# Splitting the attention maxima on GpSimd instead of VectorE, in a layer of attention and experts

## The chip, the cores and the metric

One core of a Trainium2 chip runs the whole program. The metric is the device time of one execution in microseconds (us); lower is better. The engines have their own instruction queues and meet through semaphores: TensorE (PE; its weight loads have a row of their own, PEld), VectorE (DVE), ScalarE (ACT), GpSimd (POOL), and SyncE (SP), whose queue here only issues DMAs.

## The reference

The input is 8 batches of 256 tokens with 128 channels. The layer is

```python
xn = layernorm(x)
out = x + attention(xn) + ffn(xn)
# attention: 16 heads of width 8, rotary q and k, softmax(q k^T / sqrt(8)) v, output projection
# ffn: xn + shared_mlp(xn) + the 2 best of 16 experts by a sigmoid router, weights normalised
# mlp: (silu(x @ wg) * (x @ wu)) @ wd, inner width 64
```

Everything is float32. The kernel keeps that accuracy on TensorE by cutting numbers into parts: a product of fp32r halves takes three matmuls, and q and k are each cut into three bf16 parts (six products, 48 rows for a head of width 8).

## The kernel before, in words

**Blocks.** The work is ordered by hand in blocks, `blk` from -6 to 33, each with four places `i` = 0 to 3. A block handles a quarter of a batch's heads, `q` (4 heads, one for each `i`), in three steps that lie apart: at block `q - 4` the scores are computed once to find their row maxima (`max_scores`, L488, into the two PSUM banks S1a and S1b; DVE reduces them at L903 into `mx`); at block `q` they are computed again for the exponentials (`exp_scores`, L502, into S2a and S2b; ACT takes the exponential at L657 into `probs`); at block `q + 1` the probabilities are multiplied with v (`attend`, L516). Between these lie one of 36 chunks of the expert network (two experts of a group of two batches): `up` into the banks FA and FB (L375 to L377), tanh on ACT (L669), two products on DVE (L914 into `th`, L895 into `gu`), the router's weight on POOL (L984, `gu` by `wbc`), the high part on ACT (L690, `hid_hi`), the low part on POOL (L1000, `hid_lo`), and in the next block `down` into the bank Y. Rotary sums, their splits, transpositions, projections and the router of each group are placed at blocks of their own by tables at the head of the file.

**The maxima.** The maximum must be subtracted ahead of the exponential. The kernel does this inside the second score product: `q_hat` has six more rows, which hold minus the maximum in three bf16 parts, against rows of ones in `k_hat`. A half, `h`, is two quarters (8 heads, 256 queries), so 16 maxima for each of 128 partitions. `negated_half(blk)` names the half whose last maximum was found in block `blk - 1`; it is one for each even block from -2 to 28. At that block DVE runs the four stages of `negate_maxima`, one behind the maximum of each place `i`:

- i = 0, L791: `md` part 0 = bf16(-m)
- i = 1, L794: `mrest` = -m - part 0
- i = 2, L797: part 1 = bf16(`mrest`)
- i = 3, L800: part 2 = `mrest` - part 1, and the semaphore `md_ready` rises.

Each waits until the one before is done. `md` and `mrest` are single buffers; `mx` holds two batches.

**What follows.** At place 0 of the next block (`transposed_half`) PE waits for `md_ready`, transposes `md` (L477) into the S1 bank that is next in turn, and DVE copies the 24 rows out as `mT` (L807). SP then issues the load of these rows into `q_hat` (`load_max`, L325), and at the block behind that `exp_scores` reads them. SP's queue is in order, so this load stands in one line with the loads of the heads (L318), the writes of the parts (L303) and the loads of router weights (L338, 2 MB a group).

**The order on POOL in a block:** weighting of `gu`, then at some blocks the low part of xT (L970) and a residual (L966), then at 14 places a rope split (five instructions on 128x256, L253 to L262), then `hid_lo`, and at four blocks the sum of the output (L1008). On ACT `hid_hi` stands ahead of the exponential of place 2. On PE, `max_scores` needs the S1 bank that DVE read two maxima ago.

Of the kernel before, what the change touches and what calls it, by code (L numbers as in the profile page):

```python
# [14 lines left out]
NQ = 4  # L15
# [10 lines left out]
PARTS = 3  # L26
# [49 lines left out]
def late_a(blk):  # L76

    return [(kind, of) for kind, blocks in LATE_A.items() for of, at in blocks.items() if at == blk]
# [7 lines left out]
def negated_half(blk):  # L86

    return blk // 2 + 1 if blk % 2 == 0 and blk // 2 + 1 in range(2 * B) else None


def transposed_half(blk):

    return negated_half(blk - 1)
# [38 lines left out]
def layer_kernel(nc, x, wqk, wv, bias, wout, gate_w, gate_b, swg, swu, swd, ewg, ewu, ewd,  # L132
                 cos, sin, ident, identb, iota, kones, out):
    f32, f32r, bf16, u32 = mybir.dt.float32, mybir.dt.float32r, mybir.dt.bfloat16, mybir.dt.uint32
    ALU = mybir.AluOpType
    ACT = mybir.ActivationFunctionType
    AX = mybir.AxisListType
    A_USE, B_USE, S_USE = bank_uses()
# [7 lines left out]
    with ctx:  # L146
        def sb(name, shape, dt=f32):
            return ctx.enter_context(nc.sbuf_tensor(name, shape, dt))
# [4 lines left out]
        def sem(name):  # L153
            return ctx.enter_context(nc.semaphore(name))
# [29 lines left out]
        mx = sb("mx", [P, 2, 2, SB, 2, NQ])  # L184
        mrest = sb("mrest", [P, SB * 2 * NQ])
        md = sb("md", [P, SB, 2, PARTS, NQ], bf16)
# [23 lines left out]
        stage = wbc[:, 1].rearrange("p c t -> p (c t)")  # L210
# [19 lines left out]
        md_ready = sem("md_ready")  # L230
        s1_ready, s1_read, s2_ready, exp_done = sem("s1_ready"), sem("s1_read"), sem("s2_ready"), sem("exp_done")
# [8 lines left out]
        def chunk_group(n):  # L240
            return n // NCH, n % NCH
# [460 lines left out]
        def _(dve):  # L702
            steps = [0]

            def step(instruction):

                steps[0] += 1
                instruction.then_inc(dve_step, 1)

            def settled():  # L710

                dve.wait_ge(dve_step, steps[0])
# [67 lines left out]
                                                  ALU.mult))  # L780
                    nc.vector.tensor_tensor(wtok[:], wsel[:, :, 0, :], wsel[:, :, 1, :], ALU.add).then_inc(wtok_ready, 1)

            def negate_maxima(h, stage):

                slot, half = (h // 2) % 2, h % 2
                m = mx[:, slot, half].rearrange("p t r j -> p (t r) j")
                part = [md[:, :, :, k, :].rearrange("p t r j -> p (t r) j") for k in range(PARTS)]
                left = mrest[:].rearrange("p (a j) -> p a j", j=NQ)
                if stage == 0:
                    dve.wait_ge(s1_read, S_USE["max", 2 * NQ * (h + 1) - 1] + 1)  # L790
                    step(nc.vector.tensor_scalar(part[0], m, -1.0, None, ALU.mult))  # L791
                elif stage == 1:
                    settled()
                    step(nc.vector.scalar_tensor_tensor(left, m, -1.0, part[0], ALU.mult, ALU.subtract))  # L794
                elif stage == 2:
                    settled()
                    step(nc.vector.tensor_copy(part[1], left))  # L797
                elif stage == 3:
                    settled()
                    nc.vector.tensor_tensor(part[2], left, part[1], ALU.subtract).then_inc(md_ready, 1)  # L800

            def maxima_to_rows(h):
                if h >= 2:
                    dve.wait_ge(max_ld[(h - 2) % 4], 16 * ((h - 2) // 4 + 1))
# [76 lines left out]
            for blk in range(FIRST, LAST + 1):  # L881
                n, q = blk + CHLEAD, blk + LEAD
                for g in range(1, G):
                    if NORMALISE_BLOCK.get(g) == blk:
                        normalise(g)
                for i in range(NQ):
                    if i == 0 and 0 <= n - 1 < NCHUNKS:

                        m = n - 1
                        rows = I if m % NCH == 0 else P  # L890
                        dve.wait_ge(fb_ready, B_USE["hu", m] + 1)
                        dve.wait_ge(fa_read, A_USE["hg", m] + 1)
                        if m >= 2:
                            dve.wait_ge(hid_ready, m - 1)
                        nc.vector.tensor_tensor(gu[0:rows, m % 2, :], FB[0:rows, :], th[0:rows, m % 2, :],  # L895
                                                ALU.mult).then_inc(fb_read, 1)
                    if i == 3:
                        for kind, g in late_a(blk):
                            read_a(kind, g)
                    if 0 <= q < NBLK:  # L900
                        use = S_USE["max", q * NQ + i]
                        dve.wait_ge(s1_ready, use + 1)
                        nc.vector.tensor_reduce(mx[:, (q // QB) % 2, (q // 2) % 2, :, q % 2, i],  # L903
                                                S1[use % 2][:].rearrange("p (t s) -> p t s", t=SB),
                                                axis=AX.X, op=ALU.max).then_inc(s1_read, 1)
                    if negated_half(blk) is not None:
                        negate_maxima(negated_half(blk), i)
                    if i == 0 and transposed_half(blk) is not None:
                        maxima_to_rows(transposed_half(blk))
                    if i == 0 and n < NCHUNKS:  # L910

                        rows = I if n % NCH == 0 else P
                        dve.wait_ge(th_ready, n + 1)
                        nc.vector.scalar_tensor_tensor(th[0:rows, n % 2, :], th[0:rows, n % 2, :], 1.0,  # L914
                                                       FA[0:rows, :], ALU.add, ALU.mult).then_inc(fa_read, 1)
                    if i == 1:
                        for kind, g in early_b(blk):
                            read_b(kind, g)
                    for g, stage in route_stages(blk, i):
                        route(g, stage)  # L920
# [3 lines left out]
        def _(pool):  # L924
            steps = [0]

            def after(instruction):

                steps[0] += 1
                instruction.then_inc(pool_step, 1)  # L930
                pool.wait_ge(pool_step, steps[0])
# [17 lines left out]
            def split_batch(w, g, slot):  # L949
# [3 lines left out]
                for stage in range(SPLIT_STAGES):  # L953
# [5 lines left out]
                    if stage < SPLIT_STAGES - 1:  # L959
                        pool.wait_ge(parts_done[slot], PARTS * (2 * g + w) + PART_STAGES.index(stage) + 1)  # L960

            def residual(g):
                pool.wait_ge(xn_ready, NTB * (g + 1))
                if g >= 2:
                    pool.wait_ge(out_done, 16 * (g - 1))
                nc.gpsimd.tensor_tensor(resid[:, g % 2], x_sb[:, g], xn[:, g % 2], ALU.add).then_inc(resid_ready, 1)  # L966
# [6 lines left out]
            for blk in range(FIRST, LAST + 1):  # L973
                n = blk + CHLEAD
                m = n - 1
                if 0 <= m < NCHUNKS:
                    g, c = chunk_group(m)
                    pool.wait_ge(fb_read, B_USE["hu", m] + 1)
                    if c == 0:
                        nc.gpsimd.tensor_scalar(gu[0:I, m % 2, :], gu[0:I, m % 2, :], 0.5, 1.0,  # L980
                                                ALU.mult, ALU.mult).then_inc(gu_weighted, 1)
                    else:
                        pool.wait_ge(wbc_ld[0 if c - 1 < WFIRST else 1], 32 * (g + 1))
                        nc.gpsimd.tensor_tensor(gu[:, m % 2, :], gu[:, m % 2, :], wbc[:, g % 2, c - 1, :],  # L984
                                                ALU.mult).then_inc(gu_weighted, 1)
                if blk == FIRST + 1:
                    xt_low(1)
                for kind, g in late_a(blk):
                    if kind == "G1":
                        xt_low(g)  # L990
                for g in range(G):
                    if blk == RESIDUAL_BLOCK[g]:
                        residual(g)
                for (g, w, slot), at in SPLIT_BLOCK.items():
                    if blk == at:
                        split_batch(w, g, slot)
                if 0 <= m < NCHUNKS:
                    rows = I if m % NCH == 0 else P
                    pool.wait_ge(hid_hi_ready, m + 1)
                    nc.gpsimd.tensor_tensor(hid_lo[0:rows, m % 2, :], gu[0:rows, m % 2, :],  # L1000
                                            hid_hi[0:rows, m % 2, :].bitcast(f32), ALU.subtract).then_inc(hid_ready, 1)
                for kind, g in early_b(blk):
                    if kind == "O2":
                        pool.wait_ge(fb_read, B_USE[kind, g] + 1)
                        flat = resid[:, g % 2].rearrange("p t c -> p (t c)")

                        pool.wait_ge(fa_read, A_USE["O1", min(GB * g + 1, B - 2)] + 1)
                        nc.gpsimd.tensor_tensor(flat, flat, y_tok[:], ALU.add).then_inc(o_ready, 1)  # L1008
# [61 lines left out]
```

## Time and profile before

| | |
|---|---|
| median of 3 runs | 259.78 us (257.04 to 262.89) |
| profiled execution, span | 260.4 us (no other time is given for it) |
| mean granted TensorE clock | 0.938 of full speed |
| TensorE busy | 220.3 us, 85% |
| VectorE busy | 204.7 us, 79% |
| ScalarE busy | 140.6 us, 54% |
| GpSimd busy | 157.3 us, 60% |
| DMA | 26.5 MB, mean 102 GB/s |

Busy time counts an instruction from its start to its end, also where it waits inside for something else. Instructions of one engine can overlap by up to about 0.1 us, since the next starts while the last drains. The chain that ended last is one path through the program, followed back from the end; its pieces are cut so that they don't overlap.

### The profile page before, as it was taken

The page shows a single profiled execution, that of the slowest core. Times are in us where ns is not written, and L with a number is a line of the kernel's source. Part 1 is how long each engine was busy: PE and PEld are TensorE (multiplying, and loading weights), DVE is VectorE, ACT ScalarE, POOL GpSimd, SP SyncE. Part 2 cuts the span into 40 slices and gives each one's busy share as a digit, 9 for nine tenths or more (in the row PEclk, how much of TensorE's full clock was granted, in tenths as well). Part 3 has the DMA queues.
Part 4 walks back from the last instruction along what each step waited for, and adds up shares of the span by engine and source line. Part 5 has one row for each costly group of instructions (what it writes and reads, how often), then busy time and mean ns, then how long its engine had stood idle before and what let it go on. Part 6 is the DMA issues. An engine that isn't in the chain of part 4 may idle for free.

```text
span 260.4 us, 4728 instructions
## 1 busy us (share of the span) xinstructions
PE 220.3 (85%) x1612; PEld 142.1 (55%) x1612; DVE 204.7 (79%) x468; ACT 140.6 (54%) x262; POOL 157.3 (60%) x167
## 2 busy tenths in 40 slices
PE   0572499879798986999988989999999899999973
PEld 0340265455465652666656556666766566776641
DVE  5889749949999782799996988999889789986301
ACT  2543132215566741566557656565767566676761
POOL 9299427498783545394783747469955374436711
PEclk9995569968999995999999999999999999999998
DMA  7902559440053795020235981201589611000101
GB/s 235 352 5 62 168 139 207 120 121 1 15 166 94 193 201 96 3 62 0 84 107 127 211 242 36 62 0 37 159 184 198 208 49 35 4 2 3 42 3 40
DMA packets 35183, 26.51 MB, mean 102 GB/s; under 512 B 3468, under 2 KB 29388, under 8 KB 35148
## 3 DMA queue, kind: packets, MB, share of 16 engines
q1 hardware_dynamic: 34456, 25.29, 38.4%
q10 hardware_dynamic: 704, 0.92, 1.0%
q8 instruction: 13, 0.21, 0.3%
q14 instruction: 10, 0.08, 0.1%
HBM read 18.53 MB, written 7.47 MB: 100 GB/s over the span
## 4 chain that ended last, share of the span: by engine, by line
PE 45%; DVE 26%; DMA 14%; SPq 7%; issue 5%; ACT 2%; POOL 1%; DVEq 0%; POOLq 0%
PE PV L516 8%; DVE mx L903 7%; DMA wbc<-route_w 5%; DMA q_hat<-mT 5%; PE S2b L502 4%; PE S2a L502 4%; PE S1a L488 3%; PE S1b L488 3%; PE Y L375 2%; SPq L303 2%; PE FA L376 2%; PE FA L375 2%; PE FA L377 2%; DVE xn L743 2%; PE Y L377 2%
## 5 line engine op out<-in xcount | busy, mean ns | idle before, releaser
L1000 POOL TENSOR_TENSOR hid_lo<-gu,hid_hi 128x512 fp32r<-128x512 f32 (+1 forms) x36 | 46.1, 1281 | 40.3 <-ACT hid_hi L690 40.2
L984 POOL TENSOR_TENSOR gu<-gu,wbc 128x512 f32<-128x512 f32 x32 | 40.9, 1277 | 30.3 <-DVE gu L895 22.6
L657 ACT ACTIVATE probs<-S2b 128x512 f32<-128x512 f32 x64 | 38.3, 599 | 35.0 <-PE S2b L502 34.9
L903 DVE TENSOR_REDUCE mx<-S1a 128x2 f32<-128x512 f32 x65 | 44.3, 681 | 13.2 <-PE S1a L488 13.0
L657 ACT ACTIVATE probs<-S2a 128x512 f32<-128x512 f32 x64 | 38.4, 600 | 22.3 <-PE S2a L502 20.3
L903 DVE TENSOR_REDUCE mx<-S1b 128x2 f32<-128x512 f32 x63 | 42.9, 681 | 4.9 <-PE S1b L488 4.7
L516 PE MATMUL PV<-probs,vx 128*32 128x256 f32 x512 | 35.6, 392 | 1.3 <-ACT probs L657 1.3
L669 ACT ACTIVATE th<-FA 128x512 f32<-128x512 f32 (+1 forms) x36 | 21.5, 597 | 22.0 <-PE FA L377 21.8
L690 ACT ACTIVATE hid_hi<-gu 128x512 fp32r<-128x512 f32 (+1 forms) x36 | 22.7, 632 | 13.9 <-POOL gu L984 12.7
L502 PE MATMUL S2a<-q_hat,k_hat 102*128 102x256 bf16 x128 | 25.4, 280 | 5.4 <-DMA q_hat<-mT 5.3
L914 DVE SCALAR_TENSOR_TENSOR th<-th,FA 128x512 f32<-128x512 f32 (+1 forms) x36 | 24.4, 677 | 5.8 <-ACT th L669 5.4
L895 DVE TENSOR_TENSOR gu<-FB,th 128x512 f32<-128x512 f32 (+1 forms) x36 | 24.5, 681 | 5.0 <-PE FB L377 4.9
L488 PE MATMUL S1a<-k_hat,q_hat 96*128 96x256 bf16 x130 | 25.8, 280 | 2.9 <-DVE mx L903 2.4
L488 PE MATMUL S1b<-k_hat,q_hat 96*128 96x256 bf16 x126 | 25.0, 280 | 0.8 <-DVE mx L903 0.5
L502 PE MATMUL S2b<-q_hat,k_hat 102*128 102x256 bf16 x128 | 25.2, 279 | 0.0
L375 PE MATMUL FA<-xT_hi,wg_hi 128*128 128x512 f32 (+1 forms) x36 | 18.3, 508 | 4.4 <-DVE th L914 2.3
L516 PEld LDWEIGHTS PV<-probs,vx 128*32 128x32 f32 x512 | 15.4, 110 | 12.1 <-ACT probs L657 6.1
L375 PE MATMUL FB<-xT_hi,wu_hi 128*128 128x512 f32 (+1 forms) x36 | 18.0, 500 | 3.5 <-ACT sig L615 3.2
L375 PE MATMUL Y<-hid_hi,wd_hi 128*128 128x512 f32 (+1 forms) x36 | 17.6, 490 | 1.8 <-POOL hid_lo L1000 1.8
L502 PEld LDWEIGHTS S2a<-q_hat,k_hat 102*128 102x128 bf16 x128 | 9.6, 100 | 17.1 <-DMA q_hat<-mT 6.6
L502 PEld LDWEIGHTS S2b<-q_hat,k_hat 102*128 102x128 bf16 x128 | 8.6, 98 | 18.5 <-issue 16.0
L488 PEld LDWEIGHTS S1a<-k_hat,q_hat 96*128 96x128 bf16 x130 | 11.8, 100 | 7.9 <-DVE mx L903 3.9
(128 smaller groups left out, 449.0 us busy)
## 6 DMA issues: line engine op xcount, KB each, us to landing
wbc<-route_w SPq DMA_DIRECT2D x8, 768.0 KB, 10.2
q_hat<-q_parts SPq DMA_DIRECT2D x32, 96.0 KB, 2.4
k_hat<-k_parts SPq DMA_DIRECT2D x32, 96.0 KB, 2.4
wbc<-route_w SPq DMA_DIRECT2D x8, 256.0 KB, 4.0
k_parts<-parts SPq DMA_DIRECT2D x8, 192.0 KB, 2.6
q_parts<-parts SPq DMA_DIRECT2D x8, 192.0 KB, 2.2
x_sb<-in_x SPq DMA_DIRECT2D x4, 256.0 KB, 4.0
q_parts<-parts SPq DMA_DIRECT2D x8, 128.0 KB, 2.1
```

The source lines that it names most:

```text
L375: nc.tensor.matmul(bank, w_hi, m_hi, start=start, stop=False)
L488: last = nc.tensor.matmul(bank[:, t * T:(t + 1) * T], q_hat[0:MROW, slot, pair, t * P:(t + 1) * P], k_hat[0:MROW, slot, pair, r, :], start ...
L502: last = nc.tensor.matmul(S2[head % 2][:, s * T:(s + 1) * T], k_hat[0:KALL, slot, pair, r, s * P:(s + 1) * P], q_hat[0:KALL, slot, pair, : ...
L516: last = nc.tensor.matmul(PV[32 * j:32 * j + 32, hg * T:(hg + 1) * T], vx[:, (b // GB) % 2, SB * (b % GB) + s, r, NQ * hg + j, :], probs[: ...
L657: nc.scalar.activation(probs[:, head % (2 * NQ), :], S2[head % 2][:], ACT.Exp, scale=SCALE).then_inc(exp_done, 1)
L669: nc.scalar.activation(th[0:rows, n % 2, :], FA[0:rows, :], ACT.Tanh, scale=0.5).then_inc(th_ready, 1)
L690: nc.scalar.activation(hid_hi[0:rows, (n - 1) % 2, :], gu[0:rows, (n - 1) % 2, :], ACT.Copy).then_inc(hid_hi_ready, 1)
L895: nc.vector.tensor_tensor(gu[0:rows, m % 2, :], FB[0:rows, :], th[0:rows, m % 2, :], ALU.mult).then_inc(fb_read, 1)
L903: nc.vector.tensor_reduce(mx[:, (q // QB) % 2, (q // 2) % 2, :, q % 2, i], S1[use % 2][:].rearrange("p (t s) -> p t s", t=SB), axis=AX.X, ...
L914: nc.vector.scalar_tensor_tensor(th[0:rows, n % 2, :], th[0:rows, n % 2, :], 1.0, FA[0:rows, :], ALU.add, ALU.mult).then_inc(fa_read, 1)
L984: nc.gpsimd.tensor_tensor(gu[:, m % 2, :], gu[:, m % 2, :], wbc[:, g % 2, c - 1, :], ALU.mult).then_inc(gu_weighted, 1)
L1000: nc.gpsimd.tensor_tensor(hid_lo[0:rows, m % 2, :], gu[0:rows, m % 2, :], hid_hi[0:rows, m % 2, :].bitcast(f32), ALU.subtract).then_inc(hi ...
```

## The change

The four stages leave DVE's queue. GpSimd gets `negate_maxima(h)` as the first thing in an even block, ahead of the weighting of `gu`. It has five instructions, since each of them is one plain product or sum: part 0 = bf16(-m); rest = m + part 0; part 1 = bf16(-rest); rest = rest + part 1; part 2 = bf16(-rest). The parts are the same in value. Each waits for the one before (`after`), and the last raises `md_ready`. It waits for the last maximum of the half and for the transposition of the half before, which read `md`. DVE gets a wait ahead of the first maximum of a half, for the split of the half whose place in `mx` it overwrites, four halves back.

```diff
--- before.py
+++ after.py
@@ -780,25 +780,6 @@
                                                   ALU.mult))
                     nc.vector.tensor_tensor(wtok[:], wsel[:, :, 0, :], wsel[:, :, 1, :], ALU.add).then_inc(wtok_ready, 1)
 
-            def negate_maxima(h, stage):
-
-                slot, half = (h // 2) % 2, h % 2
-                m = mx[:, slot, half].rearrange("p t r j -> p (t r) j")
-                part = [md[:, :, :, k, :].rearrange("p t r j -> p (t r) j") for k in range(PARTS)]
-                left = mrest[:].rearrange("p (a j) -> p a j", j=NQ)
-                if stage == 0:
-                    dve.wait_ge(s1_read, S_USE["max", 2 * NQ * (h + 1) - 1] + 1)
-                    step(nc.vector.tensor_scalar(part[0], m, -1.0, None, ALU.mult))
-                elif stage == 1:
-                    settled()
-                    step(nc.vector.scalar_tensor_tensor(left, m, -1.0, part[0], ALU.mult, ALU.subtract))
-                elif stage == 2:
-                    settled()
-                    step(nc.vector.tensor_copy(part[1], left))
-                elif stage == 3:
-                    settled()
-                    nc.vector.tensor_tensor(part[2], left, part[1], ALU.subtract).then_inc(md_ready, 1)
-
             def maxima_to_rows(h):
                 if h >= 2:
                     dve.wait_ge(max_ld[(h - 2) % 4], 16 * ((h - 2) // 4 + 1))
@@ -899,12 +880,12 @@
                             read_a(kind, g)
                     if 0 <= q < NBLK:
                         use = S_USE["max", q * NQ + i]
+                        if i == 0 and q % 2 == 0 and q >= 8:
+                            dve.wait_ge(md_ready, q // 2 - 3)
                         dve.wait_ge(s1_ready, use + 1)
                         nc.vector.tensor_reduce(mx[:, (q // QB) % 2, (q // 2) % 2, :, q % 2, i],
                                                 S1[use % 2][:].rearrange("p (t s) -> p t s", t=SB),
                                                 axis=AX.X, op=ALU.max).then_inc(s1_read, 1)
-                    if negated_half(blk) is not None:
-                        negate_maxima(negated_half(blk), i)
                     if i == 0 and transposed_half(blk) is not None:
                         maxima_to_rows(transposed_half(blk))
                     if i == 0 and n < NCHUNKS:
@@ -959,6 +940,21 @@
                     if stage < SPLIT_STAGES - 1:
                         pool.wait_ge(parts_done[slot], PARTS * (2 * g + w) + PART_STAGES.index(stage) + 1)
 
+            def negate_maxima(h):
+
+                slot, half = (h // 2) % 2, h % 2
+                m = mx[:, slot, half].rearrange("p t r j -> p (t r) j")
+                part = [md[:, :, :, k, :].rearrange("p t r j -> p (t r) j") for k in range(PARTS)]
+                left = mrest[:].rearrange("p (a j) -> p a j", j=NQ)
+                pool.wait_ge(s1_read, S_USE["max", 2 * NQ * (h + 1) - 1] + 1)
+                if h:
+                    pool.wait_ge(s1_ready, S_USE["M", h - 1] + 1)
+                after(nc.gpsimd.tensor_scalar(part[0], m, -1.0, 1.0, ALU.mult, ALU.mult))
+                after(nc.gpsimd.tensor_tensor(left, m, part[0], ALU.add))
+                after(nc.gpsimd.tensor_scalar(part[1], left, -1.0, 1.0, ALU.mult, ALU.mult))
+                after(nc.gpsimd.tensor_tensor(left, left, part[1], ALU.add))
+                nc.gpsimd.tensor_scalar(part[2], left, -1.0, 1.0, ALU.mult, ALU.mult).then_inc(md_ready, 1)
+
             def residual(g):
                 pool.wait_ge(xn_ready, NTB * (g + 1))
                 if g >= 2:
@@ -973,6 +969,8 @@
             for blk in range(FIRST, LAST + 1):
                 n = blk + CHLEAD
                 m = n - 1
+                if negated_half(blk) is not None:
+                    negate_maxima(negated_half(blk))
                 if 0 <= m < NCHUNKS:
                     g, c = chunk_group(m)
                     pool.wait_ge(fb_read, B_USE["hu", m] + 1)
```

## Rows read from the trace of the kernel before

**Rows 1.** the page, engine shares: PE and DVE, then the chain by engine
```profile
PE 220.3 (85%) x1612; PEld 142.1 (55%) x1612; DVE 204.7 (79%) x468; ACT 140.6 (54%) x262; POOL 157.3 (60%) x167
...
PE 45%; DVE 26%; DMA 14%; SPq 7%; issue 5%; ACT 2%; POOL 1%; DVEq 0%; POOLq 0%
```

**Rows 2.** by stretches; busy PE, PEld, DVE, ACT, POOL, clock, DMA
```profile
220.00:240.00 20.00, 20.00 (x174) 13.80 (x172) 16.28 (x33) 13.44 (x25) 10.18 (x8) 1.00 0.01 3
```

**Rows 3.** chain of waits, 60 to 69 us; columns start, length, what
```profile
61.58 0.79 DVE md L791
...
63.72 0.60 DVE mrest L794
```

**Rows 4.** chain of waits, 128 to 138 us
```profile
130.32 0.79 DVE md L791
...
134.37 1.17 DVE md L800
```

**Rows 5.** chain of waits, 168 to 174 us
```profile
168.55 0.79 DVE md L791
...
173.18 0.60 DVE md L797
```

**Rows 6.** chain of waits, 192 to 204 us
```profile
192.87 1.20 DVE md L791
...
196.54 0.86 DVE md L800
...
198.82 4.08 DMA q_hat<-mT
```

**Rows 7.** groups by line and shape, DVE; busy us, mean ns, idle
```profile
L791 DVE TENSOR_SCALAR md<-mx 128x16 bf16<-128x16 f32 x16 | 9.2, 573 | 0.0
L800 DVE TENSOR_TENSOR md<-mrest,md 128x16 bf16<-128x16 f32 x16 | 7.7, 483 | 0.0
...
L794 DVE SCALAR_TENSOR_TENSOR mrest<-mx,md 128x16 f32<-128x16 f32 x16 | 4.0, 247 | 0.0
...
L797 DVE CAST md<-mrest 128x16 bf16<-128x16 f32 x16 | 3.7, 229 | 0.0
```

**Rows 8.** timeline of POOL, 128 to 136 us; columns start, length, what
```profile
131.86 0.40 POOL L257 TENSOR_SCALAR parts<-rope 128x256 bf16<-128x256 f32 x1
132.34 0.67 POOL L259 TENSOR_TENSOR rest<-rope,parts 128x256 f32<-128x256 f32 x1
...
134.22 1.28 POOL L1000 TENSOR_TENSOR hid_lo<-gu,hid_hi 128x512 fp32r<-128x512 f32 x1
```

**Rows 9.** waits, all; columns who, for whom: us in total, times, longest
```profile
PEld S1a L477 <- DVE md L800: 4.3, 6, 1.7
...
PEld S1a L488 <- DVE mx L903: 3.9, 6, 1.3
...
PE S1a L477 <- DVE md L800: 1.7, 2, 1.3
```

**Rows 10.** groups by line and shape, POOL
```profile
L259 POOL TENSOR_TENSOR rest<-rope,parts 128x256 f32<-128x256 f32 x14 | 9.5, 679 | 1.2
...
L257 POOL TENSOR_SCALAR parts<-rope 128x256 bf16<-128x256 f32 x14 | 5.9, 422 | 1.2
...
L980 POOL TENSOR_SCALAR gu<-gu 64x512 f32<-64x512 f32 x4 | 2.5, 612 | 5.4 <-DVE gu L895 5.4
...
L934 POOL MEMSET gateb_sb<- 128x1 f32 x1 | 0.1, 98 | 0.0
```

**Rows 11.** timeline of POOL, the weighting in block 2 and in block 12
```profile
72.77 1.28 POOL L984 TENSOR_TENSOR gu<-gu,wbc 128x512 f32<-128x512 f32 x1 [0.32 <-DVE gu L895]
...
145.43 1.28 POOL L984 TENSOR_TENSOR gu<-gu,wbc 128x512 f32<-128x512 f32 x1
```

**Rows 12.** timeline of ACT, hid_hi in block 2 and in block 12
```profile
76.34 0.62 ACT L690 ACTIVATE hid_hi<-gu 128x512 fp32r<-128x512 f32 x1
...
146.74 0.63 ACT L690 ACTIVATE hid_hi<-gu 128x512 fp32r<-128x512 f32 x1 [0.90 <-POOL gu L984]
```

## The prediction

> **What bounds the kernel now.** The page first: TensorE (PE) is busy 85% of the span, VectorE (DVE) 79%, GpSimd (POOL) 60%, and the chain that ended last is 45% PE, 26% DVE, 1% POOL [rows 1]. So no engine is the bound alone. PE has the most to do, and DVE holds it up in places. In the table by stretches PE is filled completely from 220 to 240 us [rows 2]: there a faster DVE buys nothing. The chain of waits, read stretch by stretch, then says where DVE is the one that is late, and the four instructions that the change removes stand in it by name: 0.79 and 0.60 us between 60 and 69 us, 0.79 and 1.17 between 128 and 138, 0.79 and 0.60 between 168 and 174, 1.20 and 0.86 between 192 and 198 [rows 3 to 6]. Together that is 6.8 us; what else of them stands in the chain is small.
>
> Why should an instruction on 16 elements take a microsecond? The four have means of 573, 247, 229 and 483 ns, 64 instructions, 24.6 us of DVE in all [rows 7]. The long ones are waiting. The last of the four stands in the chain from 134.37 for 1.17 us, so it ends at 135.54 [rows 4]. POOL's 128x512 subtraction, begun at 134.22, took 1.28 and ended at 135.50 [rows 8]. DVE got on when POOL let go. The Trainium skill, "SBUF — State Buffer", section "Who interferes with whom", says that GpSimd and a DVE instruction that has two SBUF inputs (or runs in a two-port mode) hold one pair of ports as an exclusive lock, so that the second fully blocks; the trace agrees, by 1.17 us against POOL's end 0.04 us earlier. DVE's big instructions beside it read PSUM, and are not in this list.
>
> **The change, part by part.**
>
> *Removed from DVE.* 16 times (one for each half of a batch's heads) four instructions, and their places in the queue: the last stood behind the fourth maximum of an even block, and PE's transposition of the parts waits for it at the beginning of the next. What is that worth in time? Lower bound: the matmuls of that transposition stood idle for the last part 1.7 us in 2 places; the later of PE's two clocks on this, the weight loads, waited 4.3 us in 6 places [rows 9]. Upper bound for this term: all the big pieces of the chain, 6.8 us. I take 4.3: PE has the most work, so what PE can give is its waiting and not all of DVE's, and weight loads show a wait that the modelled end of a matmul covers. The two are not far from one another, and 4.3 lies between 1.7 and 6.8. Gain 4.3, ends 1.7 and 6.8.
>
> *Added on POOL.* Three one-input and two two-input instructions on 16 elements, each waiting for the one before. No such size is in the trace. Two-input: 679 ns for 256 elements, 1,280 for 512 [rows 8, 10], so 2.35 ns an element and about 115 ns at 16. One-input: 422 ns for 256 to bf16, 612 for 512 [rows 10], which would leave 240 ns at 16; the shortest POOL instruction of all takes 98 [rows 10]. I take the middle, 170. A dependent one starts 0.08 us after the end of the one before (131.86 + 0.40 = 132.26, next 132.34) [rows 8]. Sum: 3 x 0.17 + 2 x 0.115 + 4 x 0.08 = 1.06 us for a split. Ends: 5 x 0.098 + 0.32 = 0.8, and, if 16 elements cost what 256 do to bf16, 5 x 0.42 + 0.32 = 2.4 us.
>
> What is behind it on POOL: the weighting of gu, then ACT's hid_hi, which stands in ACT's queue ahead of the exponentials of the third and fourth pair, for which PE waits. The split begins when the last maximum of the block before is read, and in that same moment DVE begins gu, which takes 0.60 of the queue, and for which POOL has to wait anyway. So the weighting is late by 1.06 - 0.60 = about 0.5 us, and by all 1.06 where POOL comes late itself. In block 2 the weighting ends at 74.05 and hid_hi starts at 76.34 [rows 11, 12]: 2.3 us of cover, and 0.5 costs nothing. In block 12 POOL came late (it starts at 145.43 without idle time) and ACT waited 0.90 us for it [rows 11, 12]: there 1.06 us goes to the exponentials. I count half of it, 0.5, since PE has maxima and projections to do meanwhile; ends 0, and 2.1 for two such blocks with nothing hidden. The same POOL delay pushes the hid_lo subtraction and, in eight of the even blocks, the rope splits behind it; their readers (the down products, the scratch writes of SP's queue) come in general a block later, and stay covered as long as a block is over 5 us.
>
> *Waits.* POOL's new wait for the previous transposition was fulfilled a block ago. DVE's new wait before the first maximum of a half is for a split four halves back: nothing. SP's queue issues what it did, in its order; its load of the rows waits for the transposition, which comes no later. Cost of all these: 0, and under 0.1 if I am wrong in one.
>
> *A rule against it.* DVE's four were slow only beside POOL [rows 4, 7, 8]; moved there they queue behind it instead. The Trainium skill, "Perfetto Trace Analysis", section "Optimizing Scalar/DVE Operations", warns that because the two share a read port, moving work between them might not help. By it the sum would be 0, and rival 2 is that case.
>
> **Sum:** -4.3 + 0.5 = -3.8 us. The profiled span is 260.4; the page gives no time around it, and the median of the three runs, 259.8, is 0.6 below. 259.8 - 3.8 = **256.0 us**. Ends of the sum: 259.8 - 6.8 = 253.0, and 259.8 - 1.7 + 2.1 = 260.2.
>
> **Rivals.**
>
> 1. *DVE paced more than its last step shows.* The maxima behind the slow pieces come late too, and PE's weight loads for the next scores waited 3.9 us for them in 6 places [rows 9]. If that goes as well: 4.3 + 3.9 - 0.5 = 7.7, 252.1 us. For it: four of the removed stand between maxima there [rows 3, 4]. Against it: some of these waits are behind the normalisations and the routing, and PE is full from 220 on.
>
> 2. *Given back.* The stretch from 192 goes on with a load of the rows that took 4.08 us from DVE to DMA landing [rows 6], because large loads are in the DMA queues then, and not because it was asked for late. PE arrives earlier and waits longer. If the same holds for the load behind the stretch at 128, and PE absorbs the rest: 259.8 us, no change.
>
> 3. *Slower: POOL's split is expensive.* The place is the start of an even block, between the last maximum and the weighting. With x us for a split, blocks like 12 pay x each, and blocks like 2 pay x - 0.6 - 2.3. At x = 2.4 (my upper end) two blocks pay 4.8 and the gain of 4.3 is used up: 260.3. That is the point from which it decides. At x = 3.4 (0.6 an instruction, the price of 512 elements): 6.8 + 14 x 0.5 = 13.8, less 4.3, 269.3 us. Against it: it needs each instruction at over four times what the rows give for its elements.
>
> **Numbers.** Forecast 0.49 (256.0; its own range 253.5 to 258.5), rival 1 0.29 (252.1), rival 2 0.14 (259.8), rival 3 0.08 (above 260.5, mostly 262 to 269). About 2% is what a measurement of this kernel can tell from no change (the three runs lie between 257.04 and 262.89), so faster means below 254.6. Faster: nearly all of rival 1 and a sixth of the forecast, 0.36. Slower than 265.0: most of rival 3, 0.06. Same: 0.58. Range 251.0 to 260.5: it holds the forecast, rival 2 and most of rival 1, and leaves out rival 3 and the low tail.
>
> **What would show it.** Right: no instruction on md left on DVE, its busy time down by about 24 us; no wait of PE for md; POOL's five at 0.1 to 0.25 us each and 0.08 apart; the waits of weight loads for DVE's maxima smaller, those for the DMA of the rows the same or longer; ACT's hid_hi waiting for POOL only in one or two more blocks. Wrong: POOL's short instructions above 0.4 us; ACT idle before hid_hi in most even blocks; or DVE much freer while PE's idle time before 220 us stays as it was, with the DMA named in place of DVE.

## The result and the profile after

The change made the kernel faster by 1.3%: the ratio of the times after to before is 0.9874, with a 95% interval of 0.9832 to 0.9917. That is 3.3 us, against 3.8 forecast. The ratio is taken over the faster runs of each kernel (those within 1.5% of its fastest, 9 of the 20 of after); the medians of all 20 runs, 257.75 and 260.08 us, lie 2.3 us apart. In a second comparison on another chip (e5 below) the ratio was 0.9834 (0.9768 to 0.9900). The profiled execution of after has a span of 258.3 us against 260.4, 2.1 us less; single executions of this kernel differ by more than that, as the last section shows.

The page of after, the shares of the engines and the chain by engine, to be read against [rows 1]:

```profile
PE 218.8 (85%) x1612; PEld 142.0 (55%) x1612; DVE 190.1 (74%) x404; ACT 140.6 (54%) x262; POOL 173.2 (67%) x247
...
PE 42%; DMA 17%; DVE 16%; SPq 12%; POOL 6%; issue 5%; ACT 2%; POOLq 0%; DVEq 0%
```

DVE has 64 instructions fewer and its share of the chain fell from 26% to 16%. POOL has 80 more, and its share rose from 1% to 6%. DVE's busy time fell by 14.6 us and not by the 24.6 that the four had as durations [rows 7]: each of the 64 overlapped its neighbours by up to 0.1 us at either end, which the busy time counts once.

What the split costs on POOL, and what stands behind it. POOL's timeline in blocks 8 and 12 of after (start, length, what):

```profile
113.31 1.29 POOL L998 TENSOR_TENSOR hid_lo<-gu,hid_hi 128x512 fp32r<-128x512 f32 x1
114.56 0.21 POOL L952 TENSOR_SCALAR md<-mx 128x16 bf16<-128x16 f32 x1
114.86 0.22 POOL L953 TENSOR_TENSOR mrest<-mx,md 128x16 f32<-128x16 f32 x1
115.16 0.20 POOL L954 TENSOR_SCALAR md<-mrest 128x16 bf16<-128x16 f32 x1
115.45 0.22 POOL L955 TENSOR_TENSOR mrest<-mrest,md 128x16 f32<-128x16 f32 x1
115.76 0.20 POOL L956 TENSOR_SCALAR md<-mrest 128x16 bf16<-128x16 f32 x1
115.93 1.28 POOL L982 TENSOR_TENSOR gu<-gu,wbc 128x512 f32<-128x512 f32 x1
...
144.45 0.20 POOL L956 TENSOR_SCALAR md<-mrest 128x16 bf16<-128x16 f32 x1
144.62 1.29 POOL L982 TENSOR_TENSOR gu<-gu,wbc 128x512 f32<-128x512 f32 x1
```

Each instruction takes 0.20 to 0.22 us, and the next starts 0.08 to 0.09 us after its end. From 114.56 to the end of the last at 115.96 it is 1.40 us, and the weighting follows with no gap. ACT's timeline shows who pays in block 12; before, this row stood with 0.90 us of waiting [rows 12]:

```profile
145.94 0.63 ACT L690 ACTIVATE hid_hi<-gu 128x512 fp32r<-128x512 f32 x1 [2.26 <-POOL gu L982]
```

The waits of after (who, for whom: us in total, times, longest), to be read against [rows 9]:

```profile
ACT hid_hi L690 <- POOL gu L982: 16.7, 8, 4.5
...
DVE mx L886 <- PE S1a L488: 16.2, 19, 5.1
...
DVE th L895 <- ACT th L669: 10.0, 18, 1.5
...
PEld S1a L488 <- DVE mx L886: 4.4, 6, 1.8
...
PEld S1a L488 <- DMA k_hat<-k_parts: 2.8, 3, 1.3
...
PEld S1b L488 <- DVE mx L886: 1.8, 6, 0.4
```

PE's wait for `md`, 4.3 us of weight loads in 6 places, is gone: no such row is left. DVE now waits for others (10.0 us for ACT's tanh). But PE's wait for the maxima in S1a has not shrunk in this profile (3.9 us before; in the second profile of after, e5, it is 2.3), and ACT waits for the weighting in 8 places where it was 5 (12.7 us before).

Where the time came from is best seen at landmarks. Below are the times between the starts of `hid_hi` in chosen blocks, from ACT's timeline of each profile, in us:

```
blocks                   -1 to 2   2 to 6   6 to 11  11 to 14  14 to 21  21 to 24  24 to 30
before                    20.36    30.04     32.34     20.50     40.75     17.81     29.76
after                     18.70    31.47     30.74     20.57     40.54     18.10     29.74
after again (e5)          17.99    29.88     30.78     19.52     40.63     17.11     29.73
four on DVE too (e1)      18.77    30.69     32.91     20.78     41.48     17.41     29.82
four reduces too (e2)     19.43    29.59     31.92     20.70     40.55     17.31     29.82
four at once (e3)         19.77    30.08     34.12     19.61     43.35     17.66     29.92
POOL's split twice (e6)   20.82    29.37     32.79     21.29     42.99     16.80     30.87
one instruction (e10)     17.48    29.39     30.99     18.96     39.83     17.81     29.73
```

Two stretches hold the gain in both profiles of after: blocks -1 to 2 (1.7 and 2.4 us) and 6 to 11 (1.6 and 1.6 us). From block 24 on the three are the same to 0.03 us: PE is full there, as [rows 2] says. The stretches with large DMA loads (2 to 6 and 11 to 14) go either way from one execution to the next.

The first stretch can't be read without the granted clock. In blocks -1 to 2 its mean is 0.88 of full speed in before, 0.89 in after, 0.91 in e1 and 1.00 in e5; from block 6 on it is 1.00 in all eight profiles. In before PE was busy for 0.2 us of the 2 us from 53 us on, and then ran from 56 to 61 us without a gap at 0.50, the lower of the clock's two levels (1.2 GHz). In e5 that did not happen. So a part of the 2.4 us belongs to the clock and not to the change.

The time of single blocks says more, since it repeats. These are again times from one `hid_hi` to the next (e7 is the kernel before with only its router loads spread, e9 is e2 once more; both are described below):

```
block                        0      8     10   11+12     16     17
before                     7.40   7.46   7.56   13.29   7.59   5.16
before, spread (e7)        7.40   7.43   7.57   13.26   7.59   5.14
after                      5.79   6.90   6.54   13.70   7.02   5.84
after again (e5)           5.72   6.90   6.56   13.71   7.12   5.85
four on DVE too (e1)       5.88   8.03   7.53   13.73   7.97   5.83
four reduces too (e2)      6.51   8.05   6.56   13.72   7.00   5.85
the same again (e9)        5.80   8.03   6.55   13.71   7.06   5.88
four at once (e3)          8.06   8.70   8.37   13.82   8.04   5.16
```

The gain lies in four blocks: 1.6 us in block 0, 0.6 in block 8, 1.0 in block 10 and 0.5 in block 16. The price of POOL's split is seen in blocks 11 and 12 (0.4 us) and 17 (0.7; blocks 18 to 20 win back 0.35 of it together). In before PE's weight loads waited for `md` behind these same four blocks: 1.7, 0.5, 0.8 and 0.9 us.

### The profile page after: what moved, and what is told of

It is laid out like the page before. It is cut to its first block, busy times and chain, and to the rows that moved or that the text cites. A ratio compares the mean times of both kernels' runs of the same rounds, so it can differ in the third digit from the quotient of the medians.

```text
span 258.3 us, 4771 instructions
## 1 busy us (share of the span) xinstructions
PE 218.8 (85%) x1612; PEld 142.0 (55%) x1612; DVE 190.1 (74%) x404; ACT 140.6 (54%) x262; POOL 173.2 (67%) x247
## 4 chain that ended last, share of the span: by engine, by line
PE 42%; DMA 17%; DVE 16%; SPq 12%; POOL 6%; issue 5%; ACT 2%; POOLq 0%; DVEq 0%
DMA k_hat<-k_parts 9%; PE PV L516 7%; DMA wbc<-route_w 5%; SPq L318 5%; PE S2b L502 4%; SPq L303 4%; PE S1a L488 3%; DVE mx L886 3%; PE S2a L502 3%; SPq L338 3%; DVE xn L743 2%; PE Y L375 2%; PE S1b L488 2%; PE FA L375 2%; PE FA L376 2%
## 5 line engine op out<-in xcount | busy, mean ns | idle before, releaser
L895 DVE SCALAR_TENSOR_TENSOR th<-th,FA 128x512 f32<-128x512 f32 (+1 forms) x36 | 24.6, 683 | 10.7 <-ACT th L669 10.0
L876 DVE TENSOR_TENSOR gu<-FB,th 128x512 f32<-128x512 f32 (+1 forms) x36 | 24.6, 683 | 5.5 <-PE FB L377 5.4
L488 PE MATMUL S1b<-k_hat,q_hat 96*128 96x256 bf16 x126 | 24.3, 273 | 0.2
```

The lines of the kernel that those rows point to most:

```text
L488: last = nc.tensor.matmul(bank[:, t * T:(t + 1) * T], q_hat[0:MROW, slot, pair, t * P:(t + 1) * P], k_hat[0:MROW, slot, pair, r, :], start ...
```

## The experiments

All ratios are against runs of the kernel before taken beside each experiment. Theory A: the time lay in DVE's queue. Theory B: in the late `md`. Theory C: in DVE's waiting for POOL inside the four alone; by A any four more instructions cost, by C only such as wait.

**e1: the four old instructions on DVE too.** After, with this in DVE's loop behind each maximum; `negate_again` is the old four stages, writing `md_x` and `mrest_x`, which nobody reads:

```diff
+                    if negated_half(blk) is not None:
+                        negate_again(negated_half(blk), i)
```

> The kernel after, and the four old instructions run on DVE too, at their old four places and with their old waits, into tiles that nobody reads. So md is ready as early as after, and DVE's queue is as full as before. Theory A (the gain is DVE's queue: slow small instructions between the maxima): the gain is gone, ratio to before 0.998 to 1.006, DVE busy near 205 us, the four at 200 to 600 ns each. Theory B (the gain is that PE's transposition no longer waits for the last part): the gain stays, about 0.987, since nobody waits for these results.

Measured 0.9993 (0.9915 to 1.0070): the gain is gone, though `md` is as early as in after. DVE busy 206.0 us. The groups of DVE in e1 (count, busy us, mean ns, idle before):

```profile
L802 DVE TENSOR_TENSOR md_x<-mrest_x,md_x 128x16 bf16<-128x16 f32 x16 | 7.8, 487 | 0.0
L793 DVE TENSOR_SCALAR md_x<-mx 128x16 bf16<-128x16 f32 x16 | 6.3, 393 | 0.0
L796 DVE SCALAR_TENSOR_TENSOR mrest_x<-mx,md_x 128x16 f32<-128x16 f32 x16 | 6.0, 378 | 0.0
L799 DVE CAST md_x<-mrest_x 128x16 bf16<-128x16 f32 x16 | 4.3, 272 | 0.0
```

24.4 us, as in [rows 7], and nobody waits for these results. So B falls as the main cause: in blocks 8, 10 and 16 `md` is early, PE waits for DVE's other results instead, and the blocks are as long as before or longer (8.03, 7.53 and 7.97 us). Block 0 is the exception: it stays at 5.88 us, as in after, with the four on DVE. There the early `md` may be what counts, but in the same place one of the router's DVE instructions (`wsel` from `wsel` and `tsel`) took 1.29 us in before and 0.29 in e1, so e1 doesn't separate the two. e1 has POOL's split beside the old four, so equal time with before also means that what early `md` gives and what the split costs are about equal. And it can't choose between A and C, since these four do wait for POOL. Of the 64 in before 24 took over 0.3 us, and each of these 24 ended 0.02 to 0.04 us after a POOL instruction did.

**e2 and e9: four reductions on DVE instead.** The same places, but each stage is this:

```diff
+                step(nc.vector.tensor_reduce(left, m.unsqueeze(3), axis=AX.X, op=ALU.max))
```

> As the last, but the four extra instructions on DVE are tensor_reduce on the same 16 elements (one SBUF input), which I take not to wait for POOL. They cost their own time, 0.16 us each and some 0.1 of the queue. Theory C (it is the waiting for POOL's instruction inside the four that cost the time): nearly all of the gain stays, 0.987 to 0.991, and none of the four takes over 0.25 us. Theory A in its plain form (any four more instructions in the queue): 0.995 or more. By B 0.987.

> The kernel of e2 once more: its interval there (0.986 to 1.008) was too wide to choose. By theory C (the time is lost where a DVE instruction waits inside for POOL's) 0.984 to 0.989; by plain occupancy of the queue, as in e1, 0.995 or more.

Measured 0.9971 (0.9860 to 1.0081), and in e9 0.9960 (0.9900 to 1.0019), above C's range of 0.984 to 0.989. The group of them in e2:

```profile
L794 DVE TENSOR_REDUCE mrest_x<-mx 128x16 f32<-128x16 f32 x64 | 10.1, 158 | 0.1
```

None waits inside (0.158 us each, 10.1 us together), and still the ratio is nearer to e1 than to after. That alone would speak for A, but the blocks say otherwise. In blocks 10 and 16 the four reductions cost nothing (6.56 and 7.00 us, as after), where the old four of e1 cost 1.0 and 0.9 us. In block 10 two of e1's four waited for POOL, and none of e2's (DVE's timelines of e1 and of e2):

```profile
130.33 0.93 DVE L793 TENSOR_SCALAR md_x<-mx 128x16 bf16<-128x16 f32 x1
...
134.43 1.25 DVE L802 TENSOR_TENSOR md_x<-mrest_x,md_x 128x16 bf16<-128x16 f32 x1
```

```profile
129.15 0.15 DVE L794 TENSOR_REDUCE mrest_x<-mx 128x16 f32<-128x16 f32 x1
...
132.58 0.16 DVE L794 TENSOR_REDUCE mrest_x<-mx 128x16 f32<-128x16 f32 x1
```

Only in block 8 do the reductions cost as much as the old four, 1.1 us, in e2 and in e9. There the lost time is a wait for POOL too, of a neighbour: the router's cast, which took 0.15 us in after, came just behind the start of POOL's `hid_lo` in e2 and took 1.25 us (1.23 in e9). The timeline of e2, then the cast in that of after:

```profile
117.33 1.30 POOL L1013 TENSOR_TENSOR hid_lo<-gu,hid_hi 128x512 fp32r<-128x512 f32 x1
...
117.42 1.25 DVE L769 CAST topf<-topi 128x8 f32<-128x8 uint32 x1
```

```profile
118.42 0.15 DVE L767 CAST topf<-topi 128x8 f32<-128x8 uint32 x1
```

So in blocks 8, 10 and 16 time was lost only where some small DVE instruction waited for POOL. What C had wrong is that these need not be the four themselves: an added instruction that doesn't wait can shift another one into POOL's way. A cost of plain occupancy is not shown. By the ratios the reductions cost 2.2 us against after, good to about 1.9 (e9); the blocks 6 to 11 show 1.2 to 1.3 of it, and where the rest lies, if it is real, stays open.

**e3: all four stages on DVE at once.** The kernel before, with

```diff
-                    if negated_half(blk) is not None:
-                        negate_maxima(negated_half(blk), i)
+                    if i == 0 and negated_half(blk) is not None:
+                        for stage in range(4):
+                            negate_maxima(negated_half(blk), stage)
```

> The kernel before, with all four stages on DVE behind the first maximum of the even block, one after the other, in place of one behind each maximum. md is ready over three places earlier. Theory B: most of the gain, about 0.99, and no wait of PE for md. Theory A: no gain or a loss, 0.998 to 1.015, because the same slow instructions stand in the queue, and each now waits for the one before (64 waits of under 0.1 us) ahead of th, the second maximum and what PE needs next.

Measured 1.0224 (1.0111 to 1.0337), above what A had given. PE no longer waits for `md` and the kernel is 2% slower. DVE's timeline in block 10 of e3:

```profile
130.77 0.68 DVE L903 TENSOR_REDUCE mx<-S1a 128x2 f32<-128x512 f32 x1
131.37 0.86 DVE L791 TENSOR_SCALAR md<-mx 128x16 bf16<-128x16 f32 x1
132.27 0.66 DVE L794 SCALAR_TENSOR_TENSOR mrest<-mx,md 128x16 f32<-128x16 f32 x1
132.96 0.17 DVE L797 CAST md<-mrest 128x16 bf16<-128x16 f32 x1
133.17 0.25 DVE L800 TENSOR_TENSOR md<-mrest,md 128x16 bf16<-128x16 f32 x1
133.34 0.67 DVE L915 SCALAR_TENSOR_TENSOR th<-th,FA 128x512 f32<-128x512 f32 x1
133.94 0.68 DVE L903 TENSOR_REDUCE mx<-S1b 128x2 f32<-128x512 f32 x1
```

Between the first maximum and the next 1.97 us go to the four, all ahead of `th`, whose bank PE's projections want, and of the second maximum; the two long ones again end with a POOL instruction. So an early `md` isn't enough. It doesn't show that an early `md` is worth nothing, since the four in a row cost more than before at the same time.

**e4: the split on POOL behind the weighting.** After, with `negate_maxima` on POOL moved behind the weighting of `gu` and ahead of the rope split.

> The kernel after, with the split on POOL moved behind the weighting of gu. md is ready some 1.3 us later, which is still half a block ahead of its transposition. The split took 1.4 us in the trace of after, and the weighting begins that much less DVE's 0.6 us later than it could in each of 16 blocks. If that delay costs PE anything (blocks 8, 12, 18, 20 and 28, where ACT waits for the weighting): 0.5 to 1.5 us faster than after, ratio 0.981 to 0.985, and ACT's wait for the weighting down from 16.7 us to about 12. If it is all hidden: 0.987, as after.

Measured 0.9880 (0.9822 to 0.9938), as after. ACT's wait for the weighting was 18.0 us and not 12. What it wins in some blocks (0.9 us in 11 and 12 together, 0.7 in 17) it loses in others (1.2 in block 0, 0.5 in 10 and in 16, 0.7 in 18) and, 1.4 us, in block -2. POOL's timeline there:

```profile
49.40 1.28 POOL L980 TENSOR_TENSOR gu<-gu,wbc 128x512 f32<-128x512 f32 x1 [3.94 <-DMA wbc<-route_w]
50.65 0.20 POOL L952 TENSOR_SCALAR md<-mx 128x16 bf16<-128x16 f32 x1
```

The weighting waited 3.94 us for the first load of router weights, the split behind it too, and PE's weight load then 2.4 us for `md`. At the start of the block, where the change puts it, that wait hides it.

**e5: after again**, as a yardstick.

> The kernel after, unchanged, beside the kernel before and the three others of this call, so that all stand against the same runs. Ratio 0.987 if nothing else moves; it is the yardstick for the others.

Measured 0.9834 (0.9768 to 0.9900).

**e6: POOL's split twice.** The five instructions repeated on POOL behind `md_ready`, into tiles that nobody reads.

> The kernel after, with the five instructions on POOL run twice, the second time into tiles that nobody reads. md is ready as before; the weighting of gu is late by another 1.5 us in 16 blocks. If POOL's cost is as I forecast (a delay of about 0.8 us a block, hidden but in blocks like 12): the second 1.5 us is less hidden, since five even blocks have no cover left (hid_hi now starts at once behind the weighting in blocks 0, 8, 12, 18, 20, 28): 3 to 6 us slower than after, ratio 0.998 to 1.010. If POOL is nowhere near the path: 0.987 to 0.990.

Measured 1.0083 (1.0037 to 1.0129), 2.5% or 6.5 us slower than e5, just above what I expected. The chain by engine, and the waits:

```profile
PE 34%; POOL 20%; DVE 14%; DMA 12%; issue 9%; SPq 5%; ACT 4%; POOLq 0%; DVEq 0%; ACTq 0%
```

```profile
ACT hid_hi L692 <- POOL gu L991: 33.4, 21, 4.5
...
PE PV L518 <- ACT probs L659: 6.6, 7, 1.8
```

The path of rival 3 is real: weighting late, `hid_hi` late, exponentials late, and PE waits 6.6 us for them.

**e10: one of POOL's five.** After with the first instruction only; the parts 1 and 2 of the maxima are zero from the start, so the subtracted maximum has bf16 precision.

> The kernel after, with only the first of POOL's five instructions (part 0 of minus the maximum); the other two parts stay zero from the start, so the maximum that is subtracted has bf16 precision only. POOL has 1.2 us less work at the start of 16 blocks, and all else is as after. This is the price of the split on POOL, which my sum put at 0.5 us (ends 0 and 2.1). e6 showed that the next 1.5 us cost 6 us or more. If the first 1.2 us are hidden: ratio 0.982 to 0.985 (up to 0.5 us better than after). If the delay costs in proportion to e6: 0.965 to 0.972.

Measured 0.9799 (0.9750 to 0.9849), between the two ranges expected. Against e5's 0.9834 that is 0.9 us, against the 20 runs of after 2.0 us. The intervals overlap, so this is a size and no proof. The blocks agree with it: 11 and 12 take 13.17 us together (after 13.70), 16 and 17 take 11.87 (after 12.86). In the chain of e10 POOL has 2%.

**e7 and e8: router loads in two steps**, in the kernel before (e7) and in after (e8):

```diff
+ROUTE_REST_BLOCK = {1: 4, 2: 12, 3: 20}
...
                     if ROUTE_LOAD_BLOCK[g] == blk:
-                        load_route(g)
+                        load_route(g, (0,))
+                    if ROUTE_REST_BLOCK[g] == blk:
+                        load_route(g, (1,))
```

I tried this because of the end of the chain of after in blocks 4 to 6: heads issued behind the router weights land after 10.58 us, and PE waits for them until 100.28. (In before PE waited 3.54 us for the maxima rows at the same place and went on at 99.95.)

```profile
87.47 2.14 SPq L318
89.61 0.04 issue
89.66 10.58 DMA k_hat<-k_parts
100.24 0.05 issue
100.28 0.61 PE S1a L488 x2
```

> The kernel before, with each group's load of router weights issued in two steps: its first 512 KB at the old block (3, 10, 18), the other 1.5 MB one or two blocks later (4, 12, 20), behind the loads of heads and maxima rows of that block. The waits of PE for the rows and heads at 96 to 100, 152 and 200 us (PE's weight loads: 6.6 us for the rows, 1.1 for k_hat in before) should shrink to under 3. 2 to 4 us faster than before, 0.985 to 0.992, if PE cannot use the time elsewhere less.

> The same two-step load in the kernel after. Theory of the give-back (after was 2.0 us ahead at block 2 and 0.55 at block 6, where PE waited for a load behind the router weights; the DMA queue took 1.4 us back): the change is worth more without the collision, 1.5 to 2 us more than in e5, so 0.970 to 0.978 against before and 0.985 or less against e7. If the give-back is chance: as far from e7 as e5 is from before, about 0.987 of it.

Measured 0.9869 (0.9793 to 0.9944) and 0.9691 (0.9627 to 0.9755). From `hid_hi` of block 5 to that of block 6 both take 6.16 us, where before has 12.28 and after 13.16: the stall was real. By the ratio the spread loads give 3.4 us in the kernel before and not the 6.1 of this block, since in e7's profile block 23 takes 10.89 us where before has 5.76, with heads that landed after 8.18 us. After against before is 0.9691 / 0.9869 = 0.982 with the spread loads, and 0.9834 or 0.9874 without. The change is worth about the same either way within the intervals, which are wider than the 1.4 us (0.5%) in question, so these ratios don't settle whether the DMA queue takes any of it back (0.9691 lies just below the range of my theory, and 0.982 against e7 fits it as well as its rival). The second profile of after does more: in blocks 2 to 6, where the first gave back 1.4 us (31.47 against 30.04), it takes 29.88. So the loss was one of that execution and not of the change.

**e11 and e12: the last group's second step at block 19**, and in e12 also POOL's split put where POOL waits for ACT (ahead of `hid_lo`) in blocks without a rope split.

> The kernel of e8 with the second step of the last group's router load at block 19 in place of 20, ahead of the writes of the last batch's parts. In e8 PE lost about 2.9 us at block 24, waiting for heads that were behind that load. Expected 1 to 3 us faster than e8: 0.959 to 0.966 against before. If the load then collides with the maxima rows of block 20 instead: 0.969, as e8.

> As e11, and POOL's split stands, but for the first half, where it delays less: ahead of hid_lo, where POOL waits for ACT, in blocks without a rope split, and behind the weighting in the others. If the delay of the weighting in even blocks costs time (e6): 0.5 to 2 us faster than e11. If it is the later hid_lo and rope splits that count as much, the same within 0.5 us, as e4 was to after.

Measured 0.9613 (0.9556 to 0.9669) and 0.9629 (0.9578 to 0.9680). e11 is the best of all: 249.3 us. In its waits the DMA is nearly gone from PE:

```profile
PEld S1a L493 <- DMA k_hat<-k_parts: 0.4, 1, 0.4
PEld S2a L507 <- DMA q_hat<-mT: 0.4, 1, 0.4
```

e11 came out as expected. e12 is within 0.4 us of it, with intervals of about 1.3 us: the place of the split on POOL matters little (as in e4); its amount does.

## Why the prediction was right

1. *The main term, 4.3 us for DVE's queue (ends 1.7 and 6.8).* The size was right. Put the four back (e1) and the ratio goes from 0.9874 (or 0.9834) to 0.9993, 3.1 to 4.1 us; the measured gain of 3.3 us with POOL's cost added (point 3) gives 4.2 to 5.3. The reason why the four were slow was right as well, and is shown best by block 10: the old four cost 1.0 us and four reductions nothing. But 4.3 was taken from PE's waits for `md`, and in blocks 8, 10 and 16 this wait can be removed with nothing gained (e1). It was a measure of how late DVE ran, and only in block 0 perhaps itself the cause. That the two have nearly the same size is in part luck.
2. *The four pieces of the chain.* 1.39 us at 60 to 69: block 0, which gave 1.6. 1.96 at 128 to 138: block 10, which gave 1.0. The two later, 3.45 us together, stand in blocks 16 and 20: block 16 gave 0.5 us, but blocks 14 to 21 as a whole 0.2 and 0.1 in the two profiles, since block 17 pays 0.7 for POOL's split; and nothing can be told from the DMA behind them in 21 to 24. Block 8, with 0.6, was not in the chain. So the chain named most of the places and overstated the later ones.
3. *POOL's split, 1.06 us (ends 0.8 and 2.4).* It took 1.40. A one-input instruction at 16 elements takes 0.204 and not 0.17, a two-input one 0.221 and not 0.115: the line through 256 and 512 elements does not hold down to 16. Its price, put at 0.5 us (ends 0 and 2.1), is 0.9 to 2.0 for 1.2 us of it (e10). Block 12 was a right place: 0.90 us of waiting became 2.26, and blocks 11 and 12 together are 0.4 us longer. Block 17, 0.7 us longer, was not foreseen.
4. *Rival 1* (the maxima's waits go too, 252.1): its time did not come, and weight loads still wait for S1a, 4.4 us in one profile of after and 2.3 in the other, against 3.9. Its mechanism, DVE late with more than its last step, is what blocks 8, 10 and 16 show. *Rival 2* (given back to the DMA): no, the ratio is clear of 1, and the second profile of after gave nothing back. *Rival 3* (POOL slower from 2.4 us a split): its path is shown by e6, and with 2.9 us a split the kernel was 0.8% slower than before. I had put the point where the gain is used up at 2.4.
5. *The warning that moving work between DVE and GpSimd might not help* (the Trainium skill, "Perfetto Trace Analysis", section "Optimizing Scalar/DVE Operations") I had read as a gain of 0; the measurement says 3.3 us. Moved to POOL, the small instructions do not wait: all 80 took 0.194 to 0.223 us. Most of what DVE ran beside them read PSUM (`gu`, `th` and the maxima); that this is the reason is not shown.
6. *DVE's busy time down by 24 us*: it was 14.6, as told above.

## What to carry to other kernels

An instruction of 16 elements in the queue of an engine that others wait for can cost a microsecond, even when nobody needs its result soon, if it stands where it waits inside for another engine's long instruction. Look for small instructions whose duration is several times that of their shortest copy (here 0.16 and up to 1.29 us), see what ends with them, and give such work to an engine with cover. When an experiment adds or removes small instructions, look at the neighbours' durations too before the queue itself is blamed. Read the cover block by block, and stop when it is used: the first 1.4 us a block on POOL cost 1 to 2 us in all, the next 1.5 us cost 6.5. And a load issued two blocks early can be too late if a 2 MB load stands ahead of it; cutting that load in two was worth as much as the change (0.9869, 0.9793 to 0.9944).

## What the runs showed that I had not expected

The same kernel starts its steady part at different times. In two profiles of after the first load of router weights landed at different times (in after POOL's weighting waited 1.73 us for it, in e5 not at all), so that `hid_hi` of block -2 could start at 50.03 and at 47.98 us (ACT's timelines, of after and of e5):

```profile
50.03 0.63 ACT L690 ACTIVATE hid_hi<-gu 128x512 fp32r<-128x512 f32 x1 [3.64 <-POOL gu L982]
```

```profile
47.98 0.63 ACT L690 ACTIVATE hid_hi<-gu 128x512 fp32r<-128x512 f32 x1 [1.97 <-POOL gu L982]
```

2.05 us of the 6.2 between these two spans (258.3 and 252.1) are there before the first exponentials. Another 2.6 lie in blocks 2 to 6 and 11 to 14, 1.0 in 21 to 24, and 0.7 in -1 to 2, where the granted clock was 0.89 in the one and 1.00 in the other. On this kernel a single profile against another says little about a change of 1%; intervals between landmarks in stretches without large loads and at full clock repeat to 0.1 us (30.74 and 30.78, 40.54 and 40.63, 29.74 and 29.73).

A small DVE instruction with one SBUF input that is a `tensor_reduce` took 0.158 us on the mean in 64 places beside POOL (e2), where the four of e1 took 0.272 to 0.487. The Trainium skill, "SBUF — State Buffer", section "Who interferes with whom", says that such a reduction never contends with GpSimd; the runs agree: about half of the 64 ran wholly inside a POOL instruction and took 0.16 us at most.
